# A post-norm attention block followed by two local-attention layers: two buffers in place of one for the turned probabilities and the evacuated values of the second attention, and a new order of the work

## The reference

```python
x = _layernorm(x + attn(x))            # 16 heads of 64, 8 key/value groups, causal over 512, output projection + bias
x = _layernorm(x + ffn_block(x))       # on the batch of 8 x 512
# ffn_block: DEPTH = 2 layers, each:
h = shift_token(x)                     # half of the features come from the token before
q, k, v = split(h @ wqkv)              # 8 heads of 64
q, k = rotary_xpos(l2norm(q) * qs, l2norm(k) * ksc)
o = local_attention(q, k, v)           # window of 64, looks at its own window and the one before
x = x + o @ wo
h = layernorm(shift_token(x)) * lg + lb
a, g = split(h @ w1 + b1)              # hidden width 341
x = x + (a * gelu(g)) @ w2 + b2
```

## Time and profile before

| | us |
|---|---|
| median of three runs (1185.85 to 1186.21) | 1186.05 |
| the profiled execution | 1185.78 |
| its span, first to last instruction | 1183.9 |
| around the span in the profiled execution | 1.9 |

### The profile page before, as it was taken

The page is one execution under the profiler, slowest core; times in us unless marked ns, Lnnn a source line. Parts: engine busy times, 40 slices in busy tenths (PEclk is TensorE's granted clock), DMA queues, the critical chain, the costliest instruction groups (busy, mean ns, idle before and its releaser), DMA issues.

```text
span 1183.9 us, 38698 instructions
## 1 busy us (share of the span) xinstructions
PE 1163.0 (98%) x14280; PEld 857.0 (72%) x14280; DVE 1040.4 (88%) x3947; ACT 1004.0 (85%) x3078; POOL 965.3 (82%) x957
## 2 busy tenths in 40 slices
PE   9999999999999999999999999999999999999987
PEld 7677676777677776777777777777777877677665
DVE  7888988898998989999899989989899898988874
ACT  7787988889888988899888898888988889887785
POOL 3777887888789797897878987899878988798963
PEclk9999999999999999999999999999999999999999
DMA  6001001001011010100001100011101101010100
GB/s 224 19 12 25 20 22 22 18 21 23 20 27 27 13 31 20 23 21 22 22 20 23 25 18 22 21 23 26 27 4 26 27 21 23 11 27 23 26 18 18
DMA packets 31067, 31.34 MB, mean 26 GB/s; under 512 B 12576, under 2 KB 21408, under 8 KB 30752
## 3 DMA queue, kind: packets, MB, share of 16 engines
q1 hardware_dynamic: 30448, 28.08, 9.7%
q10 hardware_dynamic: 432, 0.79, 0.2%
HBM read 9.98 MB, written 2.10 MB: 10 GB/s over the span
## 4 chain that ended last, share of the span: by engine, by line
PE 90%; DVE 5%; ACT 4%; issue 1%; DMA 1%; POOL 0%; POOLq 0%; SPq 0%; DVEq 0%; ACTq 0%
PE psum L644 12%; PE psum L680 12%; PE psum L657 7%; PE psum L810 6%; PE psum L794 5%; PE psum L787 5%; PE psum L756 5%; PE psum L619 5%; PE psum L689 5%; PE psum L720 5%; PE psum L715 4%; PE psum L725 4%; PE psum L818 3%; PE psum L771 3%; PE psum L738 3%; PE psum L627 2%
## 5 line engine op out<-in xcount | busy, mean ns | idle before, releaser
L857 ACT ACTIVATE prob<-prob,negmax 128x512 f32<-128x512 f32 (+3 forms) x512 | 284.3, 558 | 11.4 <-DVE negmax L1005 10.1
L1005 DVE CUSTOM_DVE_ANT_0 prob<-psum,causal 128x512 f32<-128x512 f32 (+3 forms) x512 | 232.1, 481 | 3.5 <-PE psum L644 2.0
L1208 POOL TENSOR_SCALAR prob<-prob,rowinv 128x384 f32<-128x384 f32 (+1 forms) x256 | 160.8, 642 | 76.8 <-DVE rowinv L1011 76.6
L912 ACT ACTIVATE b_prob<-b_prob,b_negmax 128x128 f32<-128x128 f32 x512 | 198.9, 396 | 3.9 <-DVE b_negmax L1086 3.9
L1228 POOL TENSOR_TENSOR r<-r 128x512 f32<-128x512 f32 x128 | 162.6, 1274 | 37.4 <-DVE r L1044 37.2
L644 PE MATMUL psum<-k_t,q_t 64*128 64x384 f32 (+3 forms) x1024 | 178.4, 451 | 2.2 <-ACT qk_t L904 1.1
L680 PE MATMUL psum<-prob_t,v 128*64 128x256 f32 x1280 | 151.4, 381 | 0.0
L1086 DVE CUSTOM_DVE_ANT_0 b_prob<-psum,band,rnorm 128x128 f32<-128x128 f32 x512 | 146.4, 345 | 3.4 <-PE psum L756 2.1
L1211 POOL TENSOR_TENSOR prob<-prob,rowinv 128x512 f32<-128x512 f32 x96 | 98.0, 1042 | 45.8 <-DVE rowinv L1011 45.8
L657 PEld LDWEIGHTS psum<-ident,prob 64*128 64x128 f32 x2560 | 98.7, 138 | 34.7 <-issue 25.9
L864 ACT COPY prob_t<-psum 128x512 f32<-128x512 f32 (+1 forms) x176 | 95.6, 544 | 32.8 <-PE psum L657 32.6
(11 more groups left out here) (107 smaller groups left out, 2880.7 us busy)
## 6 DMA issues: line engine op xcount, KB each, us to landing
vb_mid<-vb SPq DMA_DIRECT2D x112, 128.0 KB, 2.3
x_t<-in_x_t SPq DMA_DIRECT2D x8, 256.0 KB, 3.0
x_n<-in_x SPq DMA_DIRECT2D x8, 256.0 KB, 2.8
x<-x SPq DMA_DIRECT2D x64, 31.8 KB
out<-x SPq DMA_DIRECT2D x15, 128.0 KB, 2.2
wqkv<-in_wqkv SPq DMA_DIRECT2D x1, 1536.0 KB, 11.5
x<-x SPq DMA_DIRECT2D x48, 0.2 KB
w<-in_w SPq DMA_DIRECT2D x1, 682.0 KB, 13.4
```

What stands on the lines that cost most here:

```text
L857: last = af(pr, pr, ACT.Exp, bias=negmax[:, k % 4, o:o + 1], scale=-1.0, accum_out=rowsum[:, k % 4, o:o + 1])
L912: last = af(pr, pr, ACT.Exp, bias=b_negmax[:, a, o:o + 1], scale=-1.0, accum_out=b_rowsum[:, a, o:o + 1])
L1005: vec.tensor_tensor_reduce(prob[:, k % PROBS, h, p * K:(p + 1) * K], bank[:, p * K:(p + 1) * K], causal[:, S - K:S], -E ** -0.5, 3.0e38, A ...
L1208: last = gp.tensor_scalar(pr, pr, rowinv[:, k % 4, h:h + 1], 1.0, ALU.mult, ALU.mult)
```

## The change

- `b_prob_t` and `o_t` get a second buffer, chosen by `PLACE % 2`; the copies into them now wait for `b_value` and `b_wo` of two visits before. The planner's `b_turn_p` and `b_value` steps get the same looser predecessors.
- `LATE` goes from 16 to 14. The sequence now ends: layer 0 of 28, 29, 30, 31; layer 1 of 26, 27, 28, 29, 30, 31.
- `BY_ACT` goes from 4 to 5: in place 59, which is now layer 1 of tile 27, the scaling runs on ACT in place of POOL. `BY_DVE` goes from 0 to 4: in the last four visits the query's rotation sum runs on DVE in place of POOL.
- The planner tells transposes in 64x128 (`TURN`) from matmuls in 64x128 (`HALF`): no switch between them, but 55 ns for entering `HALF` straight after `TURN`; `a_scores` is planned 54 ns shorter.
- `MARGIN` goes from (0, 50) to (200, 0), `PULL` and the table `HURRY` get other values. With all of this the lists of all five engines are made anew.

No instruction is added or taken out apart from the identity matmuls (L612), whose number follows the planned holes, and the table loads on ACT, whose number follows its order.

```diff
--- before.py
+++ after.py
@@ -33,8 +33,8 @@
 PAIRS_OF = (4, 2, 1, 1)
 PROBS, PROB_TS, V_RING = 3, 4, 6
 FLOOR = 1e-24
-BANKS, LATE = 8, 16
-SINGLES, BY_ACT, BY_DVE = 2, 4, 0
+BANKS, LATE = 8, 14
+SINGLES, BY_ACT, BY_DVE = 2, 5, 4
 
 UNITS = [(b, i, c) for b in range(B) for i in range(NT) for c in range(0, CA, PAIRS_OF[i])]
 UNIT = {u: k for k, u in enumerate(UNITS)}
@@ -96,24 +96,22 @@
        "dve": {"pe": 110, "act": 112, "dve": 100, "pool": 170, "sp": 100},
        "pool": {"pe": 60, "act": 80, "dve": 80, "pool": 130, "sp": 100},
        "sp": dict.fromkeys(("pe", "act", "dve", "pool", "sp"), 2900)}
-SWITCH, TABLES, SHY, PULL = {"128x128": 202, "64x128": 155, "128x64": 150, "64x64": 97}, 1283, 110, 0.01755
-HURRY = {("act", "a_k"): 200, ("act", "a_q"): 850, ("act", "a_turn"): 50, ("act", "a_value"): 400, ("act", "b_exp"): -300,
...
-         ("pe", "b_value"): 50, ("pe", "b_wo"): 150, ("pool", "a_deviation"): -700, ("pool", "a_norm"): 6100,
...
-MARGIN = 0, 50
+SWITCH, TABLES, SHY, PULL = {"128x128": 202, "64x128": 155, "128x64": 150, "64x64": 97}, 1283, 110, 0.01369
+HURRY = {("act", "a_exp"): -350, ("act", "a_k"): -150, ("act", "a_q"): 400, ("act", "a_turn"): 100, ("act", "a_value"): 150,
...
+         ("pool", "a_deviation"): -100, ("pool", "a_norm"): 3300, ("pool", "a_scale"): 100, ("pool", "b_deviation"): -50,
...
+MARGIN = 200, 0
 IDLE, WARM_FROM, FIRST_WARM = 900, 1e6, 10
-FULL, HALF, COLS, QUARTER = "128x128", "64x128", "128x64", "64x64"
+FULL, HALF, TURN, COLS, QUARTER = "128x128", "64x128", "64x128t", "128x64", "64x64"
+AFTER_TURN = 55
 
 
 def planned_lag(source, to):
@@ -123,6 +121,13 @@
 
 def copy_ns(engine, n):
     return {"act": 50 + 0.833 * n, "dve": 80 + 1.02 * n, "pool": 320 + 1.07 * n}[engine]
+
+
+def entry_ns(shape, entered):
+
+    if shape.rstrip("t") != entered.rstrip("t"):
+        return SWITCH[entered.rstrip("t")]
+    return AFTER_TURN if shape == TURN and entered == HALF else 0
 
 
 def make_plan():
@@ -163,7 +168,7 @@
                 k = UNIT[u]
                 prob_free = unit(k - PROBS) and ("pe", "a_turn", unit(k - PROBS))
                 prob_t_free = unit(k - PROB_TS) and ("pe", "a_value", DUO[unit(k - PROB_TS)])
-                step("pe", "a_scores", u, 1.66 * np_ * K + 64,
+                step("pe", "a_scores", u, 1.66 * np_ * K + 10,
                      [("act", "a_q", (b, i, 0)), ("dve", "a_q", (b, i, 1)), ("act", "a_k", t), prob_free], HALF,
                      [[("dve", "a_max", (*u, h))] for h in range(2)])
                 for h in range(2):
@@ -171,7 +176,7 @@
                     step("act", "a_exp", (*u, h), np_ * (0.85 * K + 277), [("dve", "a_max", (*u, h))], "exp")
                 step("dve", "a_inverse", u, 85, [("act", "a_exp", (*u, 1))])
                 step("pool", "a_scale", u, 2 * (210 + 0.895 * K) if np_ == 1 else 1998, [("dve", "a_inverse", u)])
-                step("pe", "a_turn", u, 122 * np_ * (i + 1), [("pool", "a_scale", u), prob_t_free], HALF,
+                step("pe", "a_turn", u, 122 * np_ * (i + 1), [("pool", "a_scale", u), prob_t_free], TURN,
                      [[("act", "a_turn", u)], [("dve", "a_turn", u)]])
                 step("act", "a_turn", u, copy_ns("act", np_ * K), [("pe", "a_turn", u)])
                 step("dve", "a_turn", u, copy_ns("dve", np_ * K), [("pe", "a_turn", u)])
@@ -210,7 +215,7 @@
             adder = summer(*k) if s == "q" else "pool"
             step(adder, "b_rotated_" + s, k, 1229 if adder == "pool" else 800, [("dve", "b_turn_" + s, k)])
         step("pool", "b_unit", k, 1010, [("pool", "b_inverse_k", k), ("pool", "b_rotated_k", k)])
-        step("pe", "b_turn_qk", k, 492, [("pool", "b_unit", k), (summer(*k), "b_rotated_q", k), ("pe", "b_scores", ahead)], HALF,
+        step("pe", "b_turn_qk", k, 492, [("pool", "b_unit", k), (summer(*k), "b_rotated_q", k), ("pe", "b_scores", ahead)], TURN,
              [[("act", "b_turn_qk", k)], [("dve", "b_turn_qk", k)]])
         step("act", "b_turn_qk", k, copy_ns("act", 512), [("pe", "b_turn_qk", k)])
         step("dve", "b_turn_qk", k, copy_ns("dve", 512), [("pe", "b_turn_qk", k)])
@@ -221,11 +226,11 @@
             step("act", "b_exp", (*k, s), 1555, [("dve", "b_max", (*k, s))], "exp")
         step("dve", "b_inverse", k, 110, [("act", "b_exp", (*k, 1))])
         step(scaler(*k), "b_scale", k, 1856 if scaler(*k) == "pool" else 1300, [("dve", "b_inverse", k)])
-        step("pe", "b_turn_p", k, 492, [(scaler(*k), "b_scale", k), before and ("pe", "b_value", before)], HALF, [[("act", "b_turn_p", k)], [("dve", "b_turn_p", k)]])
+        step("pe", "b_turn_p", k, 492, [(scaler(*k), "b_scale", k), before_2 and ("pe", "b_value", before_2)], TURN, [[("act", "b_turn_p", k)], [("dve", "b_turn_p", k)]])
         step("act", "b_turn_p", k, copy_ns("act", 512), [("pe", "b_turn_p", k)])
         step("dve", "b_turn_p", k, copy_ns("dve", 512), [("pe", "b_turn_p", k)])
         step("pe", "b_value", k, 931, [("act", "b_turn_p", k), ("dve", "b_turn_p", k), ("sp", "b_v", k), ("sp", "b_v", ahead)], COLS, [[("act", "b_value", k)]])
-        step("act", "b_value", k, copy_ns("act", 512), [("pe", "b_value", k), before and ("pe", "b_wo", before)])
+        step("act", "b_value", k, copy_ns("act", 512), [("pe", "b_value", k), before_2 and ("pe", "b_wo", before_2)])
         step("pe", "b_wo", k, 891, [("act", "b_value", k)], FULL, [[("dve", "b_wo", k)]])
         last_of = ("dve", "end_stats", (group_of(n - 4),)) if l else ("dve", "b_w2", (l, group_of(n - 4)))
         step("dve", "b_wo", k, 201, [("pe", "b_wo", k), last_of])
@@ -300,9 +305,8 @@
                 if e == "pe":
                     if s.frees:
                         start = max(start, by_time[len(s.frees) - 1])
-                    if s.mode.split()[0] != mode:
-                        start += SWITCH[s.mode.split()[0]]
-                        shy = SHY
+                    start += entry_ns(mode, s.mode)
+                    shy = SHY if mode.rstrip("t") != s.mode.rstrip("t") else 0
                 elif e == "act" and s.mode and s.mode != function:
                     start += TABLES
                 key = start + shy - pull * way[k] - HURRY.get((e, s.name), 0)
@@ -311,7 +315,7 @@
         _, k, start = best
         s = plan[k]
         if s.engine == "pe":
-            mode = s.mode.split()[-1]
+            mode = s.mode
             gap, spare = start - free["pe"], [x for x in range(BANKS) if bank_free[x] <= free["pe"]]
             if gap > IDLE and start > WARM_FROM and spare:
                 warm = (warmed, int((gap - 500) / 218))
@@ -411,8 +415,8 @@
         qk_t = sb("qk_t", [P, LAYERS, 2, CB, 2 * P])
         vb, vb_mid = sb("vb", [P, LAYERS, 2, INNER]), sb("vb_mid", [P, LAYERS, 3, INNER])
         b_negmax, b_rowsum, b_rowinv = sb("b_negmax", [P, 2, HB]), sb("b_rowsum", [P, 2, HB]), sb("b_rowinv", [P, 2, HB])
-        b_prob, b_prob_t = sb("b_prob", [P, 2, 2, CB, P]), sb("b_prob_t", [P, 2, 2 * CB * E])
-        o_t = sb("o_t", [P, CB, P])
+        b_prob, b_prob_t = sb("b_prob", [P, 2, 2, CB, P]), sb("b_prob_t", [P, 2, 2, 2 * CB * E])
+        o_t = sb("o_t", [P, 2, CB, P])
         x2, x3 = sb("x2", [P, LAYERS, 4, 3, E]), sb("x3", [P, 4, D])
         st_b, mv_b, ve_b, rs_b = sb("st_b", [P, 4, 12]), sb("mv_b", [P, 4, 2]), sb("ve_b", [P, 4]), sb("rs_b", [P, 4])
         x_hat, f_t = sb("x_hat", [P, GROUP, D]), sb("f_t", [P, GROUP * P])
@@ -784,14 +788,14 @@
                             h = 2 * c + s
                             o = (s * CB + c) * E
                             src = vb[:, l, n % 2, h * E:(h + 1) * E] if w else vb_mid[:, l, n % 3, h * E:(h + 1) * E]
-                            last = mm(bank[half(s), c * P + WIN * w:c * P + WIN * w + WIN], src, b_prob_t[:, w, o:o + E], start=True, stop=True)
+                            last = mm(bank[half(s), c * P + WIN * w:c * P + WIN * w + WIN], src, b_prob_t[:, PLACE[l, n] % 2, w, o:o + E], start=True, stop=True)
                 last.then_inc(b_valued, 1)
 
             def wo_b(l, n):
                 pe.wait_ge(o_ready, nth("act", "b_value", (l, n)))
                 bank, = claim("b_wo", l, n)
                 for c in range(CB):
-                    last = mm(bank[:, 0:D], o_t[:, c, :], wo[:, l, c, :], start=(c == 0), stop=(c == CB - 1))
+                    last = mm(bank[:, 0:D], o_t[:, PLACE[l, n] % 2, c, :], wo[:, l, c, :], start=(c == 0), stop=(c == CB - 1))
                 last.then_inc(wo_done, 1)
 
             def turn_f(l, g):
@@ -923,15 +927,15 @@
 
             def turn_p(l, n):
                 act.wait_ge(p_turned, nth("pe", "b_turn_p", (l, n)))
-                act.wait_ge(b_valued, nth("pe", "b_value", before(l, n)))
+                act.wait_ge(b_valued, nth("pe", "b_value", before(l, n, 2)))
                 bank, _ = banks_of("b_turn_p", l, n)
-                copy(b_prob_t[:, 0, :], bank).then_inc(bp_act, 1)
+                copy(b_prob_t[:, PLACE[l, n] % 2, 0, :], bank).then_inc(bp_act, 1)
 
             def value_b(l, n):
```

(21 more changed lines are left out.)

12 lines of the change are left out of this document (removed).

## The result

The changed kernel takes 1193.96 us (median of four runs, 1192.37 to 1195.91) against 1185.95 us: ratio 1.0067, 95% interval 1.0055 to 1.0080. It is slower by 8.0 us, where 1176.9 was forecast (9.2 faster), and it lies outside the range of 1168 to 1189. The profiled execution took 1192.37 us with a span of 1190.6.

What follows compares the result with a forecast made beforehand. PE's own work was taken to bound the body, a chain of two visits the tail. Terms -3 - 5 - 1.2 + 0 = -9.2 us took 1185.8 to 1176.6, and 0.3 to the median gave 1176.9 us; range 1168 to 1189.

Steps and rivals of the forecast that it cites:

- Second buffers by themselves: Copies of turned probabilities and values: no wait goes, since they wait for PE's own steps; 0 us.
- PE's order in the body: From 30 to 1080 us: less standing still (1.4 us) and 18 fewer shape changes (1.6 us); -3 us, ends -10 and +9.
- Rival (c): Body: the 200 ns margin breaks runs of equal shapes, so more changes and a slower kernel, 1188.4 to 1195 us; chance 0.17.
- `LATE`, -5: Two layer-1 visits move into the tail's slack, so the first attention and both chain visits end earlier; -5 us, bounds 0 and -12.4.
- first two observable steps: Signs for `LATE`: last output projections of the first attention start near 1070; tile 31's layer 0 follows 3 to 12 us later.
- `BY_ACT`, 0: Tail, place 59: ACT takes on 2.45 us of scaling, covered by its 29 us of idle time; 0 us, 2.45 without cover.
- `BY_DVE`, -1.2: Last four visits: a 1274 ns POOL sum becomes a 685 ns DVE one, two on the chain; -1.2 us, bounds 0 and -5.
- Rival (a): Tail: ACT becomes the bound, busy over 90%, and the 5 us of `LATE` are given back; 1181 to 1183.7 us, chance 0.14.
- the body's risk: Upper end for PE's order from 30 to 1080 us: a third more shape changes, +9 us.
- the filler: Identity matmuls in planned holes: they end when real work is ready; 0 us, with +1 as the far end.

Runs made afterwards that it cites:

- bufs_only: Changed kernel's program with its second buffers, but with the lists of the kernel before; 1185.76 us, ratio 0.9999.
- late16: Kernel before with two buffers, its lists up to 1030 us, its old settings behind that (LATE 16, BY_ACT 4, BY_DVE 0) with a new tail table; 1189.34 us.
- late16_margin: late16 with its last stretch planned with a margin of 200 ns towards PE and a table of its own; 1184.58 us, ratio to before 0.9989.
- the lighter run: Changed kernel, same lists, with ScalarE scaling only half of the probabilities in its five visits; 1188.57 us against 1193.96.
- after_sums_back: Changed kernel, lists otherwise fixed, with the query rotation sums of the last four visits back on GpSimd; 1199.98 us, 6.0 over the changed kernel.
- act2_margin: late16_margin with BY_ACT 2, two visits fewer scaled by ScalarE, and a table of its own; 1183.70 us, ratio to before 0.9981.

## Why the prediction was wrong, point by point

**Second buffers by themselves, 0: right.** bufs_only shows it at 0.9999. What the planner makes of them, transposes of one visit ahead of value matmuls of the one before, happens eleven times in the new body; its worth lies in the body's term.

**PE's order in the body, -3: not there.** PE stands still for 5.2 us instead of 4.1, changes of shape are 302 instead of 305 where I had priced 18 fewer, and the body alone came out at +1.2 us, in runs that overlap those of late16.

**The margin: misread.** Rival (c) held it for the danger. It is the one setting of the change that helps: -4.8 us at `LATE` 16 and -6.9 at `LATE` 14 (1193.43 to 1186.52). Its place is the tail, for which my sum had no term of it. That the time came out within rival (c)'s 1188.4 to 1195 is luck: its mechanism, more changes of shape in the body, did not happen.

**`LATE`, -5: wrong, and the largest error.** Its first two observable steps came true: the first attention ended 12 us earlier in the changed kernel (8.4 was my bound) and 3.5 with `LATE` alone, and tile 31 started 20 and 13 us earlier. The step that failed is the next one, "both visits of the chain with it". I had one visit of the chain take 49 us as before. Between the two layers of tile 31 five other visits of layer 1 now stand in `SEQUENCE`, not three: I counted four, 26 to 29, and left out 30. The lead of 19.8 us was gone when layer 1 of tile 31 started, and from there on the run-out took 6 us more (3.7 with `LATE` alone, 4.0 with the margin). I had worked out the load ("it fits, narrowly") from ScalarE's busy time alone, which leaves no room for the waits between steps; ScalarE was busy for 79% of that time, no more than before, and VectorE for 91%. In place of -5 the runs show +4.1 us, or +1.9 with the margin. That it costs is seen in three pairs of kernels (+4.1, +4.3, +1.9), each with a table of its own. Which engine's queue takes the lead away stays open: taking work off VectorE did not help, and the work taken off ScalarE brought layer 1 of tile 31 forward by only 1.4 us (1139.91 to 1138.54).

**`BY_ACT`, 0: wrong as far as known.** I covered 2.45 us with ScalarE's 29 us of idle time in the tail; but nearly half of these, about 14 us, lie behind 1160 us, in the last visit's run-out. With `BY_DVE` it cost +3.1 us at `LATE` 14. The scaling of tile 27 alone was not measured. An estimate: 0.7 to 0.9 of 2.45 us, by what work taken off ScalarE gave in the changed kernel, makes some 2 us.

**`BY_DVE`, -1.2: not borne out.** The duration was right (693 ns against 685). The worth of the move depends on the lists around it: +1.7 us in late16_margin's fixed lists, -6.0 in the changed kernel's, made for it. A table made for the sums on VectorE gave no gain over one made for GpSimd (+8.6 us). GpSimd was busy for 24.8 of 30 us from 1110 to 1140 in late16_margin and for 8.4 of 20 after that, so I can't say that its relief was worth nothing, only that no kernel here shows what it was worth.

**Rival (a)** named ScalarE as the bound, and its own sign did not come: busy over 90% between the two starts, where 79% was measured, and 5.9 us more work of ScalarE behind 1080 us (80.93 against 75.00) where it took 12. Yet ScalarE's work in the tail costs 0.7 to 0.9 of its length, as the lighter run shows. It was priced too low: it gave back the 5 us of `LATE` and stopped there, while work added to such an engine is charged too. The range ended at 1189 for the same reason: its upper end held the body's risk alone, and for the tail no term had an end above 0 except the scaling and the filler.

**The sum, as far as it goes.** `LATE` +4.1, the shift at `LATE` 14 +3.1 and the body +1.2 give 8.4; late16's distance from before is 3.4 more, and the margin takes 4.8 off, or 6.9 by the pair at `LATE` 14: 7.0 or 4.9 of the 8.0 us. The parts were measured with other tables than the changed kernel's, and lists alone move the time by several us (late16 3.6, after_sums_back 6.0), so the rest of 1.0 to 3.1 us stays open.

A version that beats both kernels is late16_margin and, 0.9 us below it, act2_margin: 1183.70 us, ratio to before 0.9981.

## What to carry to other kernels

Before work is moved behind the end of the stage that fills an engine, ask what the steps of the last chain will stand behind in each engine's list, in the stretch where the work lands and not over the whole tail; an earlier start of the last chain is worth little if the chain's own steps then stand behind more steps of others. Slack in a planned order, here 200 ns towards PE, can be worth more than a tighter plan. And compare settings of a planner only with tables made for each with the same effort, and with more than one table if the difference is a few us: here new tail lists for the same settings moved the time by 3.6 us.

## What the runs showed of the hardware

The identity matmuls hold TensorE's clock. Without them the granted clock is 0.86 between 1080 and 1200 us instead of 0.99, with 0.50 (1.2 GHz) from 1190 on, and the kernel takes 7.2 us longer, though PE then has less to do.
